# Another order of the same work in the attention and MLP pipeline of a transformer layer on one core

## The chip, the cores and the metric

The kernel runs on 1 core of one Trainium2 chip. The metric is device time of the whole execution in microseconds (us). The core has five engines that run side by side, each through its own list of instructions in order: TensorE (PE, matrix products; its weight loads are listed as PEld), VectorE (DVE), ScalarE (ACT), GpSimd (POOL) and SyncE (SP, which here issues all DMAs). They wait for one another by semaphores only.

## The reference

The input is x of 16 sequences, 1024 positions, 256 channels. Everything is float32.

```python
xn = layernorm(x)                                   # eps 1e-5
Q, K, V = (xn @ W.T + b for W, b in (q, k, v))      # 16 heads of 16 channels
Q, K = rope(Q), rope(K)
scores = where(causal, Q @ K.T / 4, -1e9)           # 1024 x 1024 per head
attn = softmax(scores) @ V @ Wo.T + bo
h = square(relu(xn @ W_fc.T))                       # 1024 hidden channels
y = h @ W_proj.T
spikes = 5 steps of a leaky threshold unit on y     # mem = 0.9 mem + y - reset
out = x + attn + mean(spikes)
```

## The kernel before

The 16 sequences are worked one after another, as 16 *intervals* and a prologue. In interval b the attention of sequence b runs, and beside it the preparation of sequence b+1: layer norm, transposes, queries and keys with rotation, and the MLP. Interval 0 is written out, 1 to 13 are a hardware loop, 14 and 15 are written out again. The prologue has no attention, and interval 15 no next sequence; both use tables of their own for the MLP (MLP_FIRST, MLP_FINAL).

An interval has 18 *steps* n = 0..17, and a step has 5 *places* (n, 0) to (n, 4). Every engine's program walks over the same 90 places, and tables say which piece of work stands at which place. So the order on each engine is fixed by hand. An engine stops at a wait, and all that stands behind it on that engine stops as well.

* Attention goes by 36 *units* of 512 score columns per interval, two per step. PE makes the scores of one half of a unit (2 heads) at the places 0, 1, 3 and 4 (function scores, L1352); I write S16.0 for the first half of unit 16. ACT takes their exponential (L758). There are 2 score buffers, so a half waits until the exponential of the half before the last one is done. POOL masks the diagonal blocks (L664). At place 2 PE multiplies the finished units of earlier steps with the values (a *run*, L1369). The run of step 15 takes (27,0), (28,0), (28,1) and (29,0), where unit 29 is masked at (14, 4).
* T: four transposes of xn into xT (L1132), split by ACT (xT_hi, L715) and DVE (xT_lo, L864) into two parts for products of float32 accuracy.
* QK u.t: the two half-array turns t of query or key block u = 0..3 (query_key, L1152), table QK_AT. DVE rotates it: two operations into rot (L883, L884), two into rot_b (L889, L890); these last two are called rot-odd here. POOL adds (sum_qk, L646), ACT copies the high part to planes (plane_qk), DVE computes the low part into rot_b (low_qk, L894), and SP stores both to memory (store_planes, L423). rot and rot_b have two buffers, u % 2: rot-odd of block 2 waits until the *store* of block 0 has landed (semaphore planes_out, L889's wait), and QK 3.0 on PE waits for rot-odd of block 2.
* SP reads the stored queries and keys back in four quads of heads, 12 + 1 DMAs each (load_ring). The third load of an interval goes to the slot that the first quad used and waits for S8.1.
* M0 to M29: turns of the MLP on PE (L1174 expands, L1183 contracts, 24 matmuls each), table MLP_AT. After an odd turn the next item h is ready: ACT relu (L750), DVE square and high part (L960, L962), POOL low part (h_lo, L656), at the place of RELU_AT, which follows from MLP_AT. M(2k) waits for the h_lo of item k-1. The sums of four items (y) are copied by DVE (take_y, L989) before the next contraction.
* POOL adds the output bias to the residual rows rs (add_bias, L641), once for each of four buffers' turns in an interval. DVE counts the spikes (L971, L974, L982).
* fin/out: PE's output projection of the sequence before (L1114), four times, each followed by DVE's finish (L909) and a DMA (store_out, L480). M2 waits for the last finish.

Of the kernel before, what the change touches and what calls it, by code (L numbers as in the profile page):

```python
# [109 lines left out]
VALUES_AT = {(0, 0): ((0, 0),), (0, 3): ((0, 1), (1, 0)), (1, 0): ((1, 1),), (1, 3): ((2, 0),), (1, 4): ((2, 1),)}  # L110
VALUES_BARE = {(0, 0): ((0, 0),), (0, 3): ((0, 1),), (1, 3): ((2, 0),), (1, 4): ((2, 1),)}
# [17 lines left out]
MLP_AT = {(6, 3): (0,), (7, 0): (1,), (7, 4): (2,), (8, 2): (3, 4), (8, 4): (5, 6), (9, 3): (7, 8), (10, 0): (9,),  # L129
# [9 lines left out]
Y_AT, Y_FIRST = {(10, 0): 0, (13, 0): 1, (16, 0): 2}, {(10, 1): 0, (13, 0): 1}  # L139
# [44 lines left out]
BIAS_HERE_AT, BIAS_NEXT_AT = {(8, 2): (0,), (10, 2): (1,)}, {(14, 2): (0,), (15, 4): (1,)}  # L184
# [28 lines left out]
def layer_kernel(nc, x, wqk, bqk, wv, bv, wfc, wproj, wo, bo, tables, consts, selectors, out):  # L213
    edges = spike_thresholds()
    with ExitStack() as ctx:
# [386 lines left out]
        def _(pool):  # L602
# [64 lines left out]
            def interval(b, att, last, more, norm, first=False, final=False, again=False):  # L667
# [3 lines left out]
                for at in ((n, place) for n in range(NSTEP) for place in range(PLACES)):  # L671
# [13 lines left out]
                    for a in BIAS_HERE_AT.get(at, ()) if att else ():  # L685
                        add_bias(b, 1, a, again)
                    for a in BIAS_NEXT_AT.get(at, ()) if more else ():
                        if first and a == 0:
                            pool.wait_ge(bias_done, 1)
                        add_bias(nb, 0, a, again)  # L690
# [20 lines left out]
        def _(act):  # L711
# [54 lines left out]
            def interval(b, att, last, more, norm, first=False, final=False, again=False):  # L766
# [5 lines left out]
                for at in ((n, place) for n in range(NSTEP) for place in range(PLACES)):  # L772
# [39 lines left out]
        def _(dve):  # L812
# [186 lines left out]
            def interval(b, att, last, more, norm, first=False, final=False, again=False, bare=False):  # L999
# [4 lines left out]
                for at in ((n, place) for n in range(NSTEP) for place in range(PLACES)):  # L1004
# [105 lines left out]
        def _(pe):  # L1110
# [267 lines left out]
            def interval(b, att, last, more, norm, first=False, final=False, again=False):  # L1378
# [6 lines left out]
                for at in ((n, place) for n in range(NSTEP) for place in range(PLACES)):  # L1385
# [115 lines left out]
```

## Time and profile before

| | |
|---|---|
| median of 3 runs | 2238.26 us (2237.26 to 2238.89) |
| the profiled execution's own time | 2238.26 us |
| its span | 2236.5 us |
| PE busy | 2107.6 us, 94% |
| ACT, DVE, POOL busy | 65%, 63%, 50% |
| chain that ended last | PE 64%, issue 10%, POOL 8%, DMA 6%, DVE 5%, ACT 3% |

The span is from the first to the last instruction; 1.8 us of the time lie around it. An interval in the middle takes 132 us, and they follow one another almost identically. Busy shares are of the span. A timeline row has start, duration, engine, line, operation, written tile<-read tiles, shapes and count; what stands in brackets is idle time of the engine before it and what ended that.

### The profile page before, as it was taken

To read this page: it belongs to the slowest core of one execution; us is meant where nothing else is said; L and a number is where in the kernel's file an instruction comes from. 1 tells how busy PE (TensorE), PEld (TensorE's weight loads), DVE (VectorE), ACT (ScalarE), POOL (GpSimd) and SP (SyncE) were. 2 spreads that over 40 slices of the span, in tenths; PEclk is the share of its full clock that TensorE was granted. 3 is DMA by queue.
4 is the path that set the end of the run, shared out by engine and by line. 5 is a ranking of instruction groups with operands and counts; after the bars stand their busy time and mean duration, and the time that the engine had idled before them with its cause. 6 is when DMAs were issued, how large, how long until landed. Compare 5 with 4: busy or idle time off the path is not lost.

```text
span 2236.5 us, 67671 instructions
## 1 busy us (share of the span) xinstructions
PE 2107.6 (94%) x25492; PEld 1511.9 (68%) x25492; DVE 1399.5 (63%) x2134; ACT 1448.7 (65%) x1673; POOL 1122.2 (50%) x1074
## 2 busy tenths in 40 slices
PE   2789999999999999999999999999999999999995
PEld 2657677676767767676776767667676776767653
DVE  5555576684757658576665856667585766857543
ACT  2276766667676666767667676676767666676662
POOL 3445454463645546354564635546464544646341
PEclk9899999999999999999999999999999999999998
DMA  3354453635445363544536455453645536354442
GB/s 127 106 157 112 134 161 92 184 109 162 119 133 169 89 195 102 153 136 116 182 88 188 120 139 150 103 184 95 185 112 137 161 92 185 109 163 119 115 111 69
DMA packets 169850, 299.97 MB, mean 134 GB/s; under 512 B 25088, under 2 KB 114944, under 8 KB 157184
## 3 DMA queue, kind: packets, MB, share of 16 engines
q1 hardware_dynamic: 169600, 296.10, 46.7%
q8 instruction: 222, 3.64, 0.7%
q14 instruction: 28, 0.23, 0.0%
HBM read 174.89 MB, written 103.28 MB: 124 GB/s over the span
## 4 chain that ended last, share of the span: by engine, by line
PE 64%; issue 10%; POOL 8%; DMA 6%; DVE 5%; ACT 3%; SPq 1%; POOLq 0%; DVEq 0%; ACTq 0%
PE pair L1369 17%; PE pair L1174 13%; PE pair L1183 10%; PE pair L1352 10%; PE pair L1152 6%; PE pair L1114 5%; DMA recip_rows<-recip_dram 5%; POOL probs L664 4%; ACT probs L758 3%; PE pair L1166 3%; POOL h_lo L656 2%; POOL rs L641 1%; DMA recip_dram<-denom 1%; DVE rs L982 1%; ACT h_sq L750 1%
## 5 line engine op out<-in xcount | busy, mean ns | idle before, releaser
L758 ACT ACTIVATE probs<-pair 128x1024 f32<-128x1024 f32 x1152 | 1146.3, 1029 | 566.5 <-PE pair L1352 565.6
L656 POOL TENSOR_TENSOR h_lo<-h_sq,h_hi 128x512 fp32r<-128x512 f32 x256 | 396.7, 1549 | 456.8 <-DVE h_hi L962 456.5
L1183 PE MATMUL pair<-wproj_hi,h_hi 64*128 64x256 f32 x2048 | 586.2, 286 | 0.1
L664 POOL TENSOR_SCALAR_AFFINE_SELECT probs<-probs 128x512 f32<-128x512 f32 x512 | 394.0, 787 | 376.6 <-ACT probs L758 374.5
L1174 PE MATMUL pair<-xT_hi,wfc_hi 64*128 64x256 f32 x2048 | 548.3, 287 | 27.6 <-DVE y_sb L989 8.2
L1183 PE MATMUL pair<-wproj_hi,h_lo 64*128 64x256 f32 x2048 | 573.1, 280 | 0.0
L1183 PE MATMUL pair<-wproj_lo,h_hi 64*128 64x256 f32 x2048 | 572.6, 280 | 0.0
L1369 PE MATMUL pair<-probs,v_sb 128*17 128x512 f32 (+3 forms) x6144 | 549.9, 489 | 13.0 <-POOL probs L664 12.1
L1174 PE MATMUL pair<-xT_lo,wfc_hi 64*128 64x256 f32 x2048 | 536.8, 280 | 0.0
L1174 PE MATMUL pair<-xT_hi,wfc_lo 64*128 64x256 f32 x2048 | 536.2, 280 | 0.0
L1352 PE MATMUL pair<-q_ring,k_ring 64*128 64x512 f32 (+3 forms) x3072 | 449.6, 359 | 18.3 <-ACT probs L758 15.4
L1174 PEld LDWEIGHTS pair<-xT_hi,wfc_hi 64*128 64x128 f32 x2048 | 358.9, 187 | 59.2 <-issue 24.4
L960 DVE TENSOR_TENSOR h_sq<-h_sq 128x512 f32<-128x512 f32 x256 | 217.1, 848 | 274.4 <-ACT h_sq L750 271.5
L1183 PEld LDWEIGHTS pair<-wproj_lo,h_hi 64*128 64x128 f32 x2048 | 383.6, 187 | 1.5
L1183 PEld LDWEIGHTS pair<-wproj_hi,h_lo 64*128 64x128 f32 x2048 | 384.0, 188 | 0.0
L1183 PEld LDWEIGHTS pair<-wproj_hi,h_hi 64*128 64x128 f32 x2048 | 382.5, 187 | 0.9 <-issue 0.3
L1352 PEld LDWEIGHTS pair<-q_ring,k_ring 64*128 64x128 f32 x3072 | 258.0, 187 | 181.8 <-ACT probs L758 114.8
L1174 PEld LDWEIGHTS pair<-xT_hi,wfc_lo 64*128 64x128 f32 x2048 | 360.0, 188 | 2.8
L1174 PEld LDWEIGHTS pair<-xT_lo,wfc_hi 64*128 64x128 f32 x2048 | 360.1, 188 | 0.0
L1369 PEld LDWEIGHTS pair<-probs,v_sb 128*17 128x17 f32 x6144 | 150.9, 97 | 289.2 <-issue 233.2
L974 DVE SCALAR_TENSOR_TENSOR count<-y_sb,count 128x512 bf16<-128x512 f32 x256 | 263.8, 1030 | 3.7
L646 POOL TENSOR_TENSOR rot<-rot,rot_b 128x1024 f32<-128x1024 f32 x64 | 153.4, 2397 | 209.0 <-DVE rot_b L890 209.0
(89 smaller groups left out, 2886.9 us busy)
## 6 DMA issues: line engine op xcount, KB each, us to landing
q_ring<-qk_dram SPq DMA_DIRECT2D x384, 128.0 KB
k_ring<-qk_dram SPq DMA_DIRECT2D x384, 128.0 KB
qk_dram<-planes SPq DMA_DIRECT2D x64, 512.0 KB, 2.8
qk_dram<-rot_b SPq DMA_DIRECT2D x64, 512.0 KB, 3.7
xn<-in_x SPq DMA_DIRECT2D x17, 1024.0 KB, 5.7
rs<-in_x SPq DMA_DIRECT2D x64, 256.0 KB, 3.0
acc_dram<-rs SPq DMA_DIRECT2D x64, 256.0 KB, 4.6
attn<-numer SPq DMA_DIRECT2D x256, 64.0 KB, 2.4
```

What stands on the lines that cost most here:

```text
L646: pool.tensor_tensor(rot[u % 2][:, :, :], rot[u % 2][:, :, :], rot_b[u % 2][:, :, :], ALU.add).then_inc(rot_sum, 1)
L656: pool.tensor_tensor(h_lo[i % HB][:, :], h_sq[i % HB][:, :], h_hi[i % HB][:, :].bitcast(F32), ALU.subtract).then_inc(h_lo_done, 1)
L664: ins = pool.affine_select(view, view, [[0, 4], [1, P]], ALU.is_ge, 0.0, base=0, channel_multiplier=-1)
L758: act.activation(probs[BUFFER[n]][:, 2 * pr:2 * pr + 2, :], pair[m % NSLOT][:, :, :], ACT.Exp, scale=SCALE).then_inc(exp_done, 1)
L960: dve.tensor_tensor(sq, sq, sq, ALU.mult).then_inc(sq_h, 1)
L974: dve.scalar_tensor_tensor(count[:, :], y, edges[s], count[:, :], ALU.is_gt, ALU.add).then_inc(spike_step, 1)
L1114: ins = pe.matmul(bank, lhsT, rhs, start=n == 0, stop=n == len(parts) - 1)
L1152: ins = pe.matmul(qk_bank[eo], w[rows, k, m], x[rows, k, cols], start=turn == 0 and n == 0, stop=turn == 1 and n == len(terms) - 1, skip_g ...
L1174: return pe.matmul(fc_bank[i % 2][:, a * T2:(a + 1) * T2], w[rows, k, m], x[rows, k, g * T2:(g + 1) * T2], start=turn == 0 and n == 0, sto ...
L1183: return pe.matmul(proj_bank[:, t * D:(t + 1) * D], h[rows, a * T2 + t * P:a * T2 + (t + 1) * P], w[rows, f, :], start=i % ITEMS_OF_GROUP ...
L1352: ins = pe.matmul(pair[m % NSLOT][:, half, to:to + width(kt, g)], k_ring[rows, slot, pr, kt * P:(kt + 1) * P], q_ring[rows, slot, pr, q0:( ...
L1369: ins = pe.matmul(pv_bank[32 * i:32 * i + VW, q0 - g * G:G], v_sb[:, kt, 4 * quad + i, :], probs[BUFFER[n]][:, i, at:at + width(kt, g)], s ...
```

## The change

Tables and the order of some calls change; no operation is added or removed, and each engine does the same work on the same data.

1. MLP_AT: turns that stood in pairs at one place (7 pairs beside M3 M4, which stay) are put at places of their own, with a score half between them, as in MLP_FIRST. RELU_AT follows. (Y_AT's first entry goes with M9 to (10, 1).)
2. QK_AT: QK 0.1 from (3, 1) to (3, 0); QK 1.0, 2.0 and 3.0 from place 3 to place 4. One value turn goes from (0, 3) to (0, 4).
3. T: the transposes stand behind the run of their step, ACT's copies at place 2 instead of 0, DVE's low part behind take_numer.
4. planes are copied at place 0 of the next step; low_qk of blocks 0 to 2 moves out of the middle of the next rotation to (4, 3), (5, 3), (6, 3).
5. SP: the third ring load goes from step 6 to step 5 and stands ahead of the output store and the store of the planes; the output store stands ahead of the planes in every step.
6. add_bias: both buffers together at (2, 4) and at (13, 4), instead of one each at (8, 2), (10, 2), (14, 2) and (15, 4).

```diff
-VALUES_AT = {(0, 0): ((0, 0),), (0, 3): ((0, 1), (1, 0)), (1, 0): ((1, 1),), (1, 3): ((2, 0),), (1, 4): ((2, 1),)}
+VALUES_AT = {(0, 0): (0, 0), (0, 3): (0, 1), (0, 4): (1, 0), (1, 0): (1, 1), (1, 3): (2, 0), (1, 4): (2, 1)}
...
-QK_AT = {(2, 4): (0, 0), (3, 1): (0, 1), (3, 3): (1, 0), (4, 0): (1, 1), (4, 3): (2, 0), (5, 0): (2, 1),
-         (5, 3): (3, 0), (6, 0): (3, 1)}
+QK_AT = {(2, 4): (0, 0), (3, 0): (0, 1), (3, 4): (1, 0), (4, 0): (1, 1), (4, 4): (2, 0), (5, 0): (2, 1),
+         (5, 4): (3, 0), (6, 0): (3, 1)}
...
-PLANE_AT = {(3, 4): 0, (4, 4): 1, (5, 4): 2, (6, 4): 3}
+PLANE_AT = {(4, 0): 0, (5, 0): 1, (6, 0): 2, (7, 0): 3}
-LOW_QK_AT = {(7, 2): 3}
+LOW_QK_AT = {(4, 3): 0, (5, 3): 1, (6, 3): 2, (7, 2): 3}
...
-MLP_AT = {(6, 3): (0,), (7, 0): (1,), (7, 4): (2,), (8, 2): (3, 4), (8, 4): (5, 6), (9, 3): (7, 8), (10, 0): (9,),
...
+MLP_AT = {(6, 4): (0,), (7, 0): (1,), (8, 0): (2,), (8, 2): (3, 4), (9, 0): (5,), (9, 3): (6,), (9, 4): (7,),
...
-BIAS_HERE_AT, BIAS_NEXT_AT = {(8, 2): (0,), (10, 2): (1,)}, {(14, 2): (0,), (15, 4): (1,)}
+BIAS_HERE_AT, BIAS_NEXT_AT = (2, 4), (13, 4)
...
+                    if att and n == 5:
+                        load_ring(b, d, 2, b * 2 * NUNIT + 2 * NU)
+                    if last and n in (5, 6, 7, 8):
+                        store_out(b - 1, d - 1, n - 5)
                     if more and n in (5, 6, 7, 8):
                         store_planes(nb, nd, n - 5)
-                    if last and n in (5, 6, 7, 8):
-                        store_out(b - 1, d - 1, n - 5)
-                    if att and n == 6:
-                        load_ring(b, d, 2, b * 2 * NUNIT + 2 * NU)
...
-                    for m in T_AT.get(n, ()) if place == 0 and (more or final) else ():
+                    for m in T_AT.get(n, ()) if place == 2 and (more or final) else ():
                         high_xT(tb, m)
...
-                        rotate(nb, u, 0, items_before(b, again) if att else None)
-                        if u:
-                            low_qk(nb, u - 1)
-                        rotate(nb, u, 1, None)
+                        for eo in range(2):
+                            rotate(nb, ROTATE_AT[at], eo, items_before(b, again) if att else None)
...
-                    for m in T_AT.get(n, ()) if place == 2 and (more or final) else ():
-                        transpose(b, tb, m, att, again)
...
                         norms(nb, first_norm_bank if first else norm_bank)
+                    for m in T_AT.get(n, ()) if place == 2 and (more or final) else ():
+                        transpose(b, tb, m, att, again)
```

**SP's DMAs in steps 1 to 8.** These are the rows of interval 0, where no output store stands between. q_ring and k_ring rows with x6 are a ring load, qk_dram rows the store of planes and rot_b. Before:

```order
L432 DMA q_ring<-qk_dram 16x2048 x6
L432 DMA k_ring<-qk_dram 16x2048 x6
L435 DMA q_ring<-shift_dram 2x2048
L423 DMA qk_dram<-planes 128x2x512
L423 DMA qk_dram<-rot_b 128x2x512
L423 DMA qk_dram<-planes 128x2x512
L423 DMA qk_dram<-rot_b 128x2x512
L432 DMA q_ring<-qk_dram 16x2048 x6
L432 DMA k_ring<-qk_dram 16x2048 x6
L435 DMA q_ring<-shift_dram 2x2048
L423 DMA qk_dram<-planes 128x2x512
```

After:

```order
L433 DMA q_ring<-qk_dram 16x2048 x6
L433 DMA k_ring<-qk_dram 16x2048 x6
L436 DMA q_ring<-shift_dram 2x2048
L433 DMA q_ring<-qk_dram 16x2048 x6
L433 DMA k_ring<-qk_dram 16x2048 x6
L436 DMA q_ring<-shift_dram 2x2048
L424 DMA qk_dram<-planes 128x2x512
L424 DMA qk_dram<-rot_b 128x2x512
L424 DMA qk_dram<-planes 128x2x512
L424 DMA qk_dram<-rot_b 128x2x512
```

The 13 DMAs of the third load now stand ahead of the stores of blocks 0 and 1 instead of behind them.

**POOL in steps 12 to 14**, interval 0. AFFINE_SELECT is a mask, h_lo the low part of an MLP item, rs the bias. Before:

```order
L656 TENSOR_TENSOR h_lo_58<-h_sq_50,h_hi_54 128x512
L664 AFFINE_SELECT probs<-probs 128x4x128
L656 TENSOR_TENSOR h_lo_59<-h_sq_51,h_hi_55 128x512
L664 AFFINE_SELECT probs<-probs 128x4x128 x2
L641 TENSOR_TENSOR rs<-rs,bo_sb 128x256 x2
L656 TENSOR_TENSOR h_lo_60<-h_sq_52,h_hi_56 128x512
L664 AFFINE_SELECT probs<-probs 128x4x128 x2
```

After:

```order
L657 TENSOR_TENSOR h_lo_58<-h_sq_50,h_hi_54 128x512
L665 AFFINE_SELECT probs<-probs 128x4x128
L657 TENSOR_TENSOR h_lo_59<-h_sq_51,h_hi_55 128x512
L642 TENSOR_TENSOR rs<-rs,bo_sb 128x256 x4
L665 AFFINE_SELECT probs<-probs 128x4x128 x2
L657 TENSOR_TENSOR h_lo_60<-h_sq_52,h_hi_56 128x512
L665 AFFINE_SELECT probs<-probs 128x4x128 x2
```

The four rs operations stand together and ahead of the masks of unit 28; the last row in both is the mask of unit 29.

**PE in steps 4 to 6**, interval 0: from the run of step 5 to QK 3.0 and the next scores. Before:

```order
L1369 MATMUL pair<-probs,v_sb 17x512 x8
L1369 MATMUL pair<-probs,v_sb 17x256 x4
L1352 MATMUL pair<-q_ring,k_ring 128x256 x4
L1152 MATMUL pair<-xT_hi,wqk_hi 128x512 x2
L1152 MATMUL pair<-xT_hi,wqk_lo 128x512 x2
L1152 MATMUL pair<-xT_lo,wqk_hi 128x512 x2
L1152 MATMUL pair<-xT_hi,wqk_hi 128x512 x2
L1152 MATMUL pair<-xT_hi,wqk_lo 128x512 x2
L1152 MATMUL pair<-xT_lo,wqk_hi 128x512 x2
L1352 MATMUL pair<-q_ring,k_ring 128x256 x4
L1352 MATMUL pair<-q_ring,k_ring 128x512 x2
```

After:

```order
L1369 MATMUL pair<-probs,v_sb 17x512 x8
L1369 MATMUL pair<-probs,v_sb 17x256 x4
L1352 MATMUL pair<-q_ring,k_ring 128x256 x8
L1152 MATMUL pair<-xT_hi,wqk_hi 128x512 x2
L1152 MATMUL pair<-xT_hi,wqk_lo 128x512 x2
L1152 MATMUL pair<-xT_lo,wqk_hi 128x512 x2
L1152 MATMUL pair<-xT_hi,wqk_hi 128x512 x2
L1152 MATMUL pair<-xT_hi,wqk_lo 128x512 x2
L1152 MATMUL pair<-xT_lo,wqk_hi 128x512 x2
L1352 MATMUL pair<-q_ring,k_ring 128x512 x2
```

Both score halves of unit 11 now stand ahead of QK 3.0, and one half behind it.

## Rows read from the trace of the kernel before

**Rows 1.** Busy time by engine of one whole interval, the seventh (busy us, instructions)

```profile
898.53:1030.75 132.22, 129.64 (x1596) 93.19 (x1595) 86.64 (x132) 89.98 (x106) 69.16 (x66) 1.00 0.50 139
```

**Rows 2.** Timeline of SP, steps 4 to 7

```profile
929.32 0.41 SPq L423 DMA_DIRECT2D qk_dram<-planes  x1
929.90 0.39 SPq L423 DMA_DIRECT2D qk_dram<-rot_b  x1
...
940.21 4.29 SPq L432 DMA_DIRECT2D q_ring<-qk_dram  x6
...
949.57 0.39 SPq L423 DMA_DIRECT2D qk_dram<-planes  x1
```

**Rows 3.** DMA issues 905 to 1037 us: KB each, median us to landing

```profile
qk_dram<-planes SPq DMA_DIRECT2D x4, 512.0 KB, 2.8
qk_dram<-rot_b SPq DMA_DIRECT2D x4, 512.0 KB, 3.6
```

**Rows 4.** Timeline of DVE, steps 4 and 5

```profile
930.54 0.69 DVE L909 TENSOR_TENSOR fin<-pair,fin 128x512 f32<-128x512 f32 x1
...
936.70 0.74 DVE L889 SCALAR_TENSOR_TENSOR rot_b<-pair,neg_bqk,table 128x512 f32<-128x512 f32 x1
```

**Rows 5.** Timeline of PE: QK 1.0, S8.1 and QK 3.0

```profile
923.04 0.50 PE L1152 MATMUL pair<-xT_hi,wqk_hi 64*128 64x512 f32 x2 [0.42 <-DVE rot_b L890]
...
926.34 0.39 PE L1352 MATMUL pair<-q_ring,k_ring 64*128 64x512 f32 x2
...
938.91 0.40 PE L1152 MATMUL pair<-xT_hi,wqk_hi 64*128 64x512 f32 x2
```

**Rows 6.** Timeline of PE: one score half between turns; M0, then two halves

```profile
909.19 0.42 PE L1352 MATMUL pair<-q_ring,k_ring 64*128 64x512 f32 x2
909.48 0.39 PE L1166 MATMUL pair<-wv_hi,xT_hi 64*128 64x256 f32 x2
...
946.99 0.28 PE L1174 MATMUL pair<-xT_hi,wfc_hi 64*128 64x256 f32 x2
...
948.42 0.64 PE L1352 MATMUL pair<-q_ring,k_ring 64*128 64x512 f32 x6
948.89 0.34 PE L1174 MATMUL pair<-xT_hi,wfc_hi 64*128 64x256 f32 x2
```

**Rows 7.** Timeline of ACT: the relu behind M21

```profile
1007.46 0.60 ACT L750 ACTIVATE h_sq<-pair 128x512 f32<-128x512 f32 x1 [0.39 <-PE pair L1183]
```

**Rows 8.** Timeline of POOL, step 14

```profile
1007.17 2.31 POOL L641 TENSOR_TENSOR rs<-rs,bo_sb 128x256 f32<-128x256 f32 x2
1009.84 1.67 POOL L656 TENSOR_TENSOR h_lo<-h_sq,h_hi 128x512 fp32r<-128x512 f32 x1 [0.36 <-DVE h_hi L962]
1011.47 2.12 POOL L664 TENSOR_SCALAR_AFFINE_SELECT probs<-probs 128x512 f32<-128x512 f32 x2
```

**Rows 9.** Timeline of PE: the run of step 15

```profile
1010.93 1.92 PE L1369 MATMUL pair<-probs,v_sb 128*17 128x512 f32 x24
1013.65 0.63 PE L1369 MATMUL pair<-probs,v_sb 128*17 128x256 f32 x8 [0.80 <-POOL probs L664]
```

**Rows 10.** Timeline of PE, steps 7 and 8: M2, and S16.0 and S16.1

```profile
955.38 0.38 PE L1174 MATMUL pair<-xT_hi,wfc_hi 64*128 64x256 f32 x1 [0.19 <-DVE fin L909]
...
957.49 0.50 PE L1352 MATMUL pair<-q_ring,k_ring 64*128 64x512 f32 x2 [0.18 <-ACT probs L758]
```

**Rows 11.** Timeline of DVE, the copy of y ahead of M10

```profile
974.59 1.67 DVE L982 SCALAR_TENSOR_TENSOR rs<-count,rs 128x512 f32<-128x512 bf16 x1
976.18 0.68 DVE L989 COPY y_sb<-pair 128x512 f32<-128x512 f32 x1
```

**Rows 12.** Busy time and granted clock (PEclk, behind POOL) around an idle PE and after

```profile
51.00:55.00 4.00, 0.05 (x4) 0.04 (x2) 3.86 (x5) 0.37 (x1) 0.01 (x1) 0.90 0.11 41
55.00:60.00 5.00, 4.94 (x22) 3.46 (x24) 0.00 (x0) 2.00 (x2) 5.00 (x2) 0.50 0.48 177
...
2122.70:2126.10 3.40, 3.40 (x25) 0.62 (x16) 0.78 (x1) 0.81 (x1) 3.03 (x5) 0.50 0.00 0
```

More of the change, by code:

```diff
@@ L109 @@
 PLACES = 5
-VALUES_AT = {(0, 0): ((0, 0),), (0, 3): ((0, 1), (1, 0)), (1, 0): ((1, 1),), (1, 3): ((2, 0),), (1, 4): ((2, 1),)}
-VALUES_BARE = {(0, 0): ((0, 0),), (0, 3): ((0, 1),), (1, 3): ((2, 0),), (1, 4): ((2, 1),)}
+VALUES_AT = {(0, 0): (0, 0), (0, 3): (0, 1), (0, 4): (1, 0), (1, 0): (1, 1), (1, 3): (2, 0), (1, 4): (2, 1)}
+VALUES_BARE = {(0, 0): (0, 0), (0, 3): (0, 1), (1, 3): (2, 0), (1, 4): (2, 1)}
 TAKE_V_AT = {(0, 3): (0,), (1, 0): (1,), (1, 4): (2, 3)}
@@ L138 @@
              (13, 3): (13,), (14, 0): (14,), (14, 3): (15,), (15, 0): (16,), (15, 3): (17,)}
-Y_AT, Y_FIRST = {(10, 0): 0, (13, 0): 1, (16, 0): 2}, {(10, 1): 0, (13, 0): 1}
+Y_AT, Y_FIRST = {(10, 1): 0, (13, 0): 1, (16, 0): 2}, {(10, 1): 0, (13, 0): 1}
 Y_FINAL = {(11, 3): 2, (15, 3): 3}
@@ L684, in interval @@
                         h_low(item, i)
[L685 to L688, printed above, removed]
+                    if att and at == BIAS_HERE_AT:
+                        for a in range(2):
+                            add_bias(b, 1, a, again)
+                    if more and at == BIAS_NEXT_AT:
+                        if first:
                             pool.wait_ge(bias_done, 1)
-                        add_bias(nb, 0, a, again)
+                        for a in range(2):
+                            add_bias(nb, 0, a, again)
             root(0)
@@ L1011, in interval @@
                         take_numer(b - 1, *NUMER_AT[n], last)
-                    for m in T_AT.get(n, ()) if place == 2 and (more or final) else ():
-                        low_xT(tb, m)
                     if att and n and place == 2 and n in NUMER_AT:
@@ L1019, in interval @@
                         divide(b - 1, 1)
+                    for m in T_AT.get(n, ()) if place == 2 and (more or final) else ():
+                        low_xT(tb, m)
                     if more and at in ROTATE_AT:
-                        u = ROTATE_AT[at]
-                        if first and u == 0:
+                        if first and ROTATE_AT[at] == 0:
                             dve.wait_ge(table_in, 16)
                             dve.wait_ge(consts_done, 2)
-                        rotate(nb, u, 0, items_before(b, again) if att else None)
-                        if u:
-                            low_qk(nb, u - 1)
-                        rotate(nb, u, 1, None)
+                        for eo in range(2):
+                            rotate(nb, ROTATE_AT[at], eo, items_before(b, again) if att else None)
                     if last and place == 2 and n in O_AT:
@@ L1388, in interval @@
                         scores(b, 2 * n + place // 3, place % 3, last, more)
-                    for m in T_AT.get(n, ()) if place == 2 and (more or final) else ():
-                        transpose(b, tb, m, att, again)
                     if last and at == (0, 2):
@@ L1398, in interval @@
                         norms(nb, first_norm_bank if first else norm_bank)
+                    for m in T_AT.get(n, ()) if place == 2 and (more or final) else ():
+                        transpose(b, tb, m, att, again)
                     if last and place == 2 and n in O_AT:
                         output(b - 1, O_AT[n])
-                    for m, turn in values_at.get(at, ()) if att else ():
+                    if att and at in values_at:
+                        m, turn = values_at[at]
                         if carried and m < CARRIED:
```

7 rows, old and new, of the table MLP_AT are left out of this document.

## The prediction, made before the changed kernel ran

> **What bounds the kernel now.** I read the page first: PE busy 94%, no other engine above 65%. Then one interval of the middle by busy time: PE works 129.6 of 132.2 us at a granted clock of 1.00 [rows 1], so its idle time is only 2.6 us. PE's own order of work is the bound, and no engine beside it is near it. What the change does to PE is then two things: whether its pieces fit together more or less tightly, and whether a wait that is now covered comes uncovered. Third, I went through PE's timeline of that interval and took the distance from each piece's start to the next. A piece that is not kept waiting has always the same length: M0 goes from 946.99 to 948.42, which is 1.43 us [rows 6], and so does every MLP turn; runs, outputs and QK turns have theirs. All that stands above these lengths is about 5 us an interval. The largest waits are 0.6 us ahead of QK 1.0 (0.42 of it shown as idle, behind rot_b) [rows 5], 0.6 us ahead of M2 for the last finish and 0.4 us ahead of S16.1 [rows 10], 1.1 us ahead of M10 for the copy of y [rows 11], and 1.0 us inside the run of step 15 for a mask [rows 9]. So even an order without any waits could not win more than 5 us x 15 = 75 us. Fourth, since PE waits for DVE, DVE for stores, and SP issues them in order, I read SP's timeline.
>
> Times below are those of the seventh interval, with the changed order laid over them. The tables changed act in intervals 0 to 14, so each term counts 15 times.
>
> **The third ring load ahead of the stores.** It can't start before S8.1, which is at 926.34 and takes 0.4 us [rows 5]; in the new order about 0.3 us later by the pieces ahead of it, so the issue starts at about 927.1. How long does SP take for it? In the trace the load starts at 940.21 and the next DMA behind it at 949.57: 9.36 us for 13 DMAs [rows 2]. The output store (its finish is done by 931.2 [rows 4]) comes next, and each issue takes 0.58 us (929.32 to 929.90 [rows 2]). So planes go out at 937.1 and rot_b at 937.7, and rot_b lands after 3.6 us [rows 3]: 941.3. Before, the same store was issued at 929.32 and had landed by 933.5. Rot-odd of block 2 waits for this landing; it started at 936.70 and takes two operations of 0.7 us, 1.4 us [rows 4]. It will now start at 941.4 and end at 942.8. QK 3.0 started at 938.91 [rows 5] and with the score half put ahead of it would be due at 939.3. It waits 3.5 us. Queued behind rot-odd on DVE are a copy of the numerator, the finish of output 1, low_qk 1 and the rotation of block 3; on POOL the sum of block 2; all of them are needed only behind QK 3.0, so they move along and add 0.2 us at most (M0 waits for block 3). Term: +3.5 us, from 0 (if the store came through in time) to 5 (if the ring's data delays its landing).
>
> Moving low_qk 0 behind the finish at 930.54 [rows 4] would alone be hidden: done at 932.5, issued at once, landed at 936.9, two tenths behind 936.70 and ahead of 939.3.
>
> Here the Trainium skill speaks for the change. "DMA: Bandwidth & Descriptors", in its rules for kernel authors, says to issue a DMA early and wait for it late. By that rule the earlier ring load costs nothing, and the sum would be 3.5 us an interval lower. The same page, on the anatomy of one DMA, gives some 50 ns for the dispatch by the issuing sequencer (for GpSimd's path); 13 of them would be 0.7 us, with the same result. This case's rows show 0.7 us for each DMA of a ring load on SP, 9.36 us in all [rows 2].
>
> **Pairs of turns taken apart.** On PE the 72 score halves stand in 50 groups now and in 59 then. A group of one half between turns takes 0.29 us (909.19 to 909.48), a group of two 0.47 us (948.42 to 948.89) [rows 6]; ahead of a run one half takes 0.32. So each group more costs 0.11 to 0.19 us. 9 x 0.15 = +1.35 us (1.0 to 1.7).
>
> **The run of step 15.** Its last part needs the mask of unit 29, which on POOL stands behind the low part of item 11, which begins with M21. M21 ends at 1007.3, its relu starts at 1007.46 [rows 7], h_lo ends at 1011.5, the mask at 1013.6 [rows 8], and the last part of the run starts at 1013.65 [rows 9]. That chain of 6.3 us stays. But between M21 and the run one MLP turn fewer stands then (M22 alone, where M22 and M23 stood): 1.43 us less cover. Term at least +1.4. And POOL now does both bias pairs behind h_lo 10. A pair took 2.31 us [rows 8]. Counting from the end of M19: h_lo 10 done at 3.5, bias at 8.1, the two masks of unit 28 at 9.8, h_lo 11 at 11.5, mask 29 at 13.6, run done at 14.2; without a wait it would be done at 10.2. That is 4.0 us of waiting, against 1.0 before: +3.0. If the pairs take less, as they should with DVE less busy, nearer to 1.4. I take the middle, +2.2 us.
>
> **Three score halves in a row.** M2 goes behind S16.0 and M5 behind S18.0. The third half in a row must wait for an exponential (0.93 to 1.03 us) of the first. For M2: S16.0 comes about 1.0 us late, while the 0.6 us for the finish and the 0.4 us for S16.1 [rows 10] are gone: 0. For M5: S18.0 about 1.1 us late; the 0.4 us ahead of M6 (h_lo 2) goes. Together +0.8 us (0 to 1.5).
>
> **Transposes behind the run.** The chain transpose, xT_hi, xT_lo, QK 0.0 has lost the run's 2.28 us as cover and keeps QK 0.0 waiting 0.9 us. Then QK 1.0, whose rotation hangs on the reciprocal's DMA and comes at 923.0 whatever PE does, no longer waits 0.6 us [rows 5], and a 0.3 us wait ahead of QK 0.1 goes. Term 0 (-0.3 to +0.5).
>
> **The copy of y.** It waited behind a 1.67 us operation on rs that ended late (974.59, copy at 976.18 [rows 11]); in the new order one score half more lies between, and DVE is through. -0.5 us (-0.6 to 0). The bias at (2, 4) is hidden: POOL would wait there for the rotation of block 0, and the four operations (4.6 us at most [rows 8]) end about when that does; half a microsecond more would only delay a sum that is due a step later.
>
> Sum per interval: 3.5 + 1.35 + 2.2 + 0.8 + 0 - 0.5 = 7.35 us; x 15 = 110 us.
>
> **The clock.** In the middle of the kernel the clock was granted in full [rows 1]. PE now gets a hole of 3.5 us. Where PE stood still for 4 us in the prologue (51 to 55), the clock fell to 0.50, that is 1.2 GHz, and the turns after it ran at that [rows 12]; and in interval 15, where PE's waits are longer than in the middle ones, there is a stretch of 3.4 us at 0.50 [rows 12]. 3.4 us at half speed do the work of 1.7, so a fall costs up to 1.7 us. The seventh interval, with waits of 1 us at most, has none [rows 1]. I take one fall per interval, mostly behind QK 3.0: +1.5 us (0 to 3.4, if the run of step 15 brings another), x 15 = 22 us.
>
> Own time of the profiled execution 2238.3 (span 2236.5 and 1.8 around it), which is the median of the runs: 2238.3 + 110 + 22 = **2370 us**.
>
> **Rivals.**
> - *No fall of the clock.* For it: no stall of the middle intervals had one. Against: none was this long. 2238.3 + 110 = 2348 us.
> - *The ring load doesn't hold up the stores*, the case of the rule above: if SP gets through it sooner, or the landing is in time. For: rot-odd is only due at 937.9, and the DMA engines are only half busy [rows 1]. Against: 9.36 us of issue. Sum 7.35 - 3.5 = 3.85 us, no hole, no fall of the clock: 2296 us.
> - *Both waits at their upper end*: ring data delays the landing (+1.5), the bias holds the mask (+0.8), and the clock falls twice (+1.7): 13 us an interval, 2430 us.
> - *Faster.* Turns spread evenly give the chain behind each turn more time, and the waits of today go: 0.6 + 0.6 + 0.4 + 0.4 + 0.5 + 1.0 = 3.5 us, less 1.0 for the groups: -2.5 us x 15, 2201 us. It needs the store in time, and it is decided at step 15: the mask would have to be done before the run gets to it, 3 us earlier than I count. Against: the chain of M21 is 6.3 us by rows, and the cover I count is less than it.
>
> **How the numbers follow.** Forecast 0.40, no fall 0.27, ring load harmless 0.16, upper end 0.08, faster 0.04, nearly nothing 0.02, and 0.03 for something slower that I don't see. The likeliest is 2370 us. The range goes from 2293 (ring load harmless) to 2402 and leaves out the upper end and the faster side. A change of 0.2% (4.5 us) is about what can be told here. Slower by more: 0.94; within: 0.02; faster: 0.04.
>
> **What would show it.** In the changed profile rot-odd of block 2 should be released by a DMA (qk_dram<-planes or rot_b) and QK 3.0 by it, with 3 to 4 us of idle PE in every interval and a step 5 near 12 us; SP should show planes of block 0 issued some 10 us behind S8.1. The run of step 15 should take over 4.5 us, released by POOL. PEclk should fall below 1.00 in the middle slices. I am wrong if the planes are stored in time, or if DVE shows no wait there; and if intervals stay near 132 us, the view that PE's waits are the price of the order is wrong.

## The result and the profile after

| | before | changed |
|---|---|---|
| median | 2238.57 us | 2439.39 us (2433.15 to 2440.19, 4 runs) |
| span of the profiled execution | 2236.5 us | 2434.8 us |
| mean granted clock | 0.988 | 0.962 |
| PE busy | 94% | 90% |

The ratio is 1.089, with a 95% interval of 1.087 to 1.091. The change costs 201 us, 13.4 us for each of 15 intervals (12.4 us in the seventh, 975.10 to 1119.71). The forecast was 2370 us with a range to 2402: the sign was right, the size half as large again as forecast.

The span in 40 slices, busy tenths of PE: first the row of the page before, then two rows of the changed kernel's page, PE and tenths of the granted clock:

```profile
PE   2789999999999999999999999999999999999995
```

```profile
PE   3889999898989989999898989989999898999985
PEclk9899999999999999999999999999999999999998
```

PE's row, which was all nines in the middle, has eights now. The clock's row has nines as before: tenths of a slice are too coarse for what the mean clock shows. From 0.988 to 0.962 is 131 us more at half speed (0.038 x 2434.8 x 2 = 185 us, less 0.012 x 2236.5 x 2 = 54 us). At half speed that is work worth up to 66 us. PE's busy time grew by 77 us (2107.6 to 2184.2) and its idle time by 122 us (128.9 to 250.6).

The waits that grew, over the whole trace of the changed kernel (total us, times, longest us):

```profile
DVE rot_b L892 <- DMA qk_dram<-rot_b: 121.5, 31, 7.8
...
PE pair L1152 <- DVE rot_b L893: 79.6, 18, 6.4
```

Before, the first did not occur, and the second was this:

```profile
PE pair L1152 <- DVE rot_b L890: 18.4, 16, 4.0
```

The groups of the page, with idle time behind the second bar, show the other two places: the run (L1369) and the score halves (L1352). Before:

```profile
L1369 PE MATMUL pair<-probs,v_sb 128*17 128x512 f32 (+3 forms) x6144 | 549.9, 489 | 13.0 <-POOL probs L664 12.1
...
L1352 PE MATMUL pair<-q_ring,k_ring 64*128 64x512 f32 (+3 forms) x3072 | 449.6, 359 | 18.3 <-ACT probs L758 15.4
```

Changed:

```profile
L1369 PE MATMUL pair<-probs,v_sb 128*17 128x512 f32 (+3 forms) x6144 | 556.9, 492 | 43.5 <-POOL probs L665 41.1
...
L1352 PE MATMUL pair<-q_ring,k_ring 64*128 64x512 f32 (+3 forms) x3072 | 473.0, 360 | 41.9 <-ACT probs L761 41.8
```

**The ring load and the store, steps 4 and 5 of the seventh interval.** SP's timeline of the changed kernel, which answers to [rows 2]:

```profile
1004.03 3.85 SPq L433 DMA_DIRECT2D q_ring<-qk_dram  x6
1008.06 3.80 SPq L433 DMA_DIRECT2D k_ring<-qk_dram  x6
1012.04 0.52 SPq L436 DMA_DIRECT2D q_ring<-shift_dram  x1
1012.79 0.41 SPq L481 DMA_DIRECT2D out<-fin  x1
1013.64 0.40 SPq L424 DMA_DIRECT2D qk_dram<-planes  x1
1014.22 0.37 SPq L424 DMA_DIRECT2D qk_dram<-rot_b  x1
```

DVE's timeline in that stretch (low_qk of block 0, then rot-odd of block 2), to [rows 4]:

```profile
1008.20 1.64 DVE L897 TENSOR_TENSOR rot_b<-rot,planes 128x1024 fp32r<-128x1024 f32 x1
...
1019.55 0.75 DVE L892 SCALAR_TENSOR_TENSOR rot_b<-pair,neg_bqk,table 128x512 f32<-128x512 f32 x1 [6.77 <-DMA qk_dram<-rot_b]
```

PE's, from the score halves of unit 11 to QK 3.0, to [rows 5]:

```profile
1015.70 0.74 PE L1352 MATMUL pair<-q_ring,k_ring 64*128 64x256 f32 x8
1021.01 0.79 PE L1152 MATMUL pair<-xT_hi,wqk_hi 64*128 64x512 f32 x2 [4.58 <-DVE rot_b L893]
```

Read them from the bottom. PE stands still for 4.58 us. DVE has stood still for 6.77 us before that, for a store. SP had the data at 1009.84, when low_qk ended, but it was in the middle of 13 DMAs and issued the store at 1013.64. From the last issue to the release are 5.3 us (1014.22 to 1019.55), where I had counted 3.6. From the load's first row to the release are 15.5 us, where I had counted 14.2 (927.1 to 941.3).

**The run of step 15.** POOL's timeline, to [rows 8], and PE's, to [rows 9]:

```profile
1088.16 2.19 POOL L657 TENSOR_TENSOR h_lo<-h_sq,h_hi 128x512 fp32r<-128x512 f32 x1 [1.65 <-DVE h_hi L965]
1090.31 3.46 POOL L642 TENSOR_TENSOR rs<-rs,bo_sb 128x256 f32<-128x256 f32 x4
1093.72 1.86 POOL L665 TENSOR_SCALAR_AFFINE_SELECT probs<-probs 128x512 f32<-128x512 f32 x2
1095.55 1.70 POOL L657 TENSOR_TENSOR h_lo<-h_sq,h_hi 128x512 fp32r<-128x512 f32 x1
1097.21 2.13 POOL L665 TENSOR_SCALAR_AFFINE_SELECT probs<-probs 128x512 f32<-128x512 f32 x2
```

```profile
1094.47 2.22 PE L1369 MATMUL pair<-probs,v_sb 128*17 128x512 f32 x24
1099.39 1.06 PE L1369 MATMUL pair<-probs,v_sb 128*17 128x256 f32 x8 [2.69 <-POOL probs L665]
```

POOL has no idle time from h_lo 10 to the mask of unit 29: h_lo 10, the four bias operations, masks, h_lo 11, masks. That chain ends at 1099.3. From the run's start to the next score half (1094.47 to 1100.37) are 5.9 us, where it was 3.3 us (1010.93 to 1014.20).

**The clock.** Stretches of the changed kernel behind the two holes (columns as in [rows 12]; the clock is the third number from the end):

```profile
1020.70:1024.10 3.40, 3.09 (x14) 2.24 (x16) 3.40 (x4) 0.00 (x0) 3.06 (x2) 0.51 0.23 77
...
1099.20:1102.60 3.40, 3.21 (x26) 2.29 (x28) 1.29 (x2) 1.02 (x1) 0.13 (x1) 0.51 0.65 188
```

There are two falls in this interval, and read in stretches of 3 us the trace shows these two in each of the 15 intervals. I had forecast one. The chip granted 1.2 GHz behind the 4.58 us without matmuls and behind the 2.69 us in the run.

### The profile page after: what moved, and what is told of

Same layout as the page of the kernel before. It is cut to its first block and busy times, and to the rows that moved or that the text cites. A ratio compares the mean times of both kernels' runs of the same rounds, so it can differ in the third digit from the quotient of the medians.

```text
span 2434.8 us, 67671 instructions
## 1 busy us (share of the span) xinstructions
PE 2184.2 (90%) x25492; PEld 1553.9 (64%) x25492; DVE 1431.1 (59%) x2134; ACT 1462.3 (60%) x1673; POOL 1122.6 (46%) x1074
## 5 line engine op out<-in xcount | busy, mean ns | idle before, releaser
L657 POOL TENSOR_TENSOR h_lo<-h_sq,h_hi 128x512 fp32r<-128x512 f32 x256 | 382.7, 1495 | 614.1 <-DVE h_hi L965 613.7
L1183 PE MATMUL pair<-wproj_hi,h_hi 64*128 64x256 f32 x2048 | 604.3, 295 | 0.1
L1369 PE MATMUL pair<-probs,v_sb 128*17 128x512 f32 (+3 forms) x6144 | 556.9, 492 | 43.5 <-POOL probs L665 41.1
L665 POOL TENSOR_SCALAR_AFFINE_SELECT probs<-probs 128x512 f32<-128x512 f32 x512 | 417.6, 833 | 358.8 <-ACT probs L761 358.7
L1174 PE MATMUL pair<-xT_hi,wfc_hi 64*128 64x256 f32 x2048 | 563.1, 294 | 16.0 <-DVE y_sb L992 5.3
L1174 PE MATMUL pair<-xT_lo,wfc_hi 64*128 64x256 f32 x2048 | 545.3, 285 | 0.0
L1352 PE MATMUL pair<-q_ring,k_ring 64*128 64x512 f32 (+3 forms) x3072 | 473.0, 360 | 41.9 <-ACT probs L761 41.8
L1174 PEld LDWEIGHTS pair<-xT_hi,wfc_hi 64*128 64x128 f32 x2048 | 368.5, 192 | 56.5 <-issue 17.7
L1352 PEld LDWEIGHTS pair<-q_ring,k_ring 64*128 64x128 f32 x3072 | 265.4, 190 | 186.7 <-ACT probs L761 111.3
L963 DVE TENSOR_TENSOR h_sq<-h_sq 128x512 f32<-128x512 f32 x256 | 196.5, 767 | 302.1 <-ACT h_sq L753 301.0
L1174 PEld LDWEIGHTS pair<-xT_hi,wfc_lo 64*128 64x128 f32 x2048 | 369.3, 193 | 5.1
L1369 PEld LDWEIGHTS pair<-probs,v_sb 128*17 128x17 f32 x6144 | 149.7, 97 | 329.1 <-issue 229.4
L977 DVE SCALAR_TENSOR_TENSOR count<-y_sb,count 128x512 bf16<-128x512 f32 x256 | 293.7, 1147 | 4.7
```

What stands on the lines that cost most here:

```text
L657: pool.tensor_tensor(h_lo[i % HB][:, :], h_sq[i % HB][:, :], h_hi[i % HB][:, :].bitcast(F32), ALU.subtract).then_inc(h_lo_done, 1)
L665: ins = pool.affine_select(view, view, [[0, 4], [1, P]], ALU.is_ge, 0.0, base=0, channel_multiplier=-1)
L963: dve.tensor_tensor(sq, sq, sq, ALU.mult).then_inc(sq_h, 1)
L977: dve.scalar_tensor_tensor(count[:, :], y, edges[s], count[:, :], ALU.is_gt, ALU.add).then_inc(spike_step, 1)
L1174: return pe.matmul(fc_bank[i % 2][:, a * T2:(a + 1) * T2], w[rows, k, m], x[rows, k, g * T2:(g + 1) * T2], start=turn == 0 and n == 0, sto ...
L1183: return pe.matmul(proj_bank[:, t * D:(t + 1) * D], h[rows, a * T2 + t * P:a * T2 + (t + 1) * P], w[rows, f, :], start=i % ITEMS_OF_GROUP ...
```

## The experiments

All were timed against the kernel before; two of them are variants of the changed kernel. In the expectations "Theory A" is the account of the prediction, sized with the changed kernel's trace: a store queued on SP behind a ring load, a mask that PE reaches too soon, and a clock that falls behind the holes.

### Change 5 alone

```diff
+                    if att and n == 5:
+                        load_ring(b, d, 2, b * 2 * NUNIT + 2 * NU)
+                    if last and n in (5, 6, 7, 8):
+                        store_out(b - 1, d - 1, n - 5)
                     if more and n in (5, 6, 7, 8):
                         store_planes(nb, nd, n - 5)
-                    if last and n in (5, 6, 7, 8):
-                        store_out(b - 1, d - 1, n - 5)
-                    if att and n == 6:
-                        load_ring(b, d, 2, b * 2 * NUNIT + 2 * NU)
```

> The kernel before with change 5 alone: SP issues the third ring load at step 5, ahead of the output store and the store of the planes. Theory A (the queue): rotation of block 2 waits for a store that is issued 9 us late. By the changed kernel's trace (planes issued 9.6 us behind the load's start, 5.2 us from the last issue to the release) rot-odd of block 2 ends about 4.7 us after QK 3.0 is due, and the clock falls behind the hole: +6 to +7 us an interval, 2330 to 2345 us. Rival B (the wait comes from low_qk being moved behind the finish, and the ring load is hidden): below +1 us an interval, under 2255 us.

Measured: 2334.0 us, ratio 1.043 (1.041 to 1.044), +95 us. Its SP, DVE, PE and clock:

```profile
961.07 4.95 SPq L432 DMA_DIRECT2D q_ring<-qk_dram  x6
966.20 3.80 SPq L432 DMA_DIRECT2D k_ring<-qk_dram  x6
...
972.37 0.37 SPq L423 DMA_DIRECT2D qk_dram<-rot_b  x1
```

```profile
976.12 0.75 DVE L889 SCALAR_TENSOR_TENSOR rot_b<-pair,neg_bqk,table 128x512 f32<-128x512 f32 x1 [5.23 <-DMA qk_dram<-rot_b]
```

```profile
977.58 0.80 PE L1152 MATMUL pair<-xT_hi,wqk_hi 64*128 64x512 f32 x2 [4.41 <-DVE rot_b L890]
```

```profile
977.58:982.00 4.42, 4.42 (x22) 3.59 (x24) 1.14 (x2) 1.03 (x2) 2.37 (x1) 0.50 0.51 177
```

Here low_qk stands where it did before, and the hole is as large. So SP's new order alone is sufficient; rival B falls. Of the 95 us, 57 are more idle time of PE (128.9 to 185.7 us) and 38 more busy time (2107.6 to 2146.0). The mean clock of 0.971 is 82 us more at half speed, worth up to 41, so the fall behind the hole is enough to account for the busy part.

The store lands sooner here than in the changed kernel: 3.75 us from the last issue (972.37) to the release (976.12), and 3.6 to 3.9 us in 13 of the 15 intervals, against 4.5 to 5.8 there in all but the first. It stands behind the same 13 DMAs. So the long landing in the changed kernel does not come of the ring load ahead of it alone; what else makes it was not found. In return SP took longer to issue here (5.13 us for the first six, 4.03 there), and from the load's first row to the release are 15.1 us.

### The changed kernel without change 5

> The changed kernel with SP's order of before (changes 1 to 4 and 6 stay). Theory A: the 4.7 us hole ahead of QK 3.0 and the fall of the clock behind it go, 6 to 7 us an interval: 2335 to 2350 us. Rival B: nearly all of the hole stays, over 2420 us.

Measured: 2367.0 us, ratio 1.058 (1.056 to 1.059). Taking change 5 out gives back 72 us, less than the 89 to 104 of theory A, and far more than rival B allows. The hole ahead of QK 3.0 is gone, but DMAs still release waits (whole trace):

```profile
DVE rot_b L890 <- DMA qk_dram<-rot_b: 65.5, 30, 3.1
...
ACT h_sq L751 <- DMA qk_dram<-rot_b: 21.4, 15, 2.7
```

Behind the first of these waits PE stands ahead of M0 (0.73 us in the seventh interval):

```profile
PE pair L1173 <- DVE rot_b L891: 16.4, 16, 3.1
```

There was a second instance of the same mechanism, which changes 2 and 4 alone show below. In the changed kernel PE's wait ahead of M0 for rot_b occurs twice in the whole trace, and the relu's wait for a DMA three times (3.5 us in all): with change 5 the hole ahead of QK 3.0 takes their place.

### Change 1 alone, the turns apart

> The kernel before with change 1 alone (the MLP turns of the changed kernel, relu and h_lo follow). Theory A: more groups of score halves (+1.0 to 1.4 us), M2 and M5 behind a third half (+0.8), M10's wait shorter (-0.5), and in the run of step 15 one turn less of cover (+1.4), with no more than 1.7 for a fall of the clock: +2.5 to +5 us an interval, 2275 to 2315 us. Rival (even spacing helps and the bias makes the wait of step 15): +0 to +1 us an interval, under 2255 us.

Measured: 2303.6 us, ratio 1.029 (1.028 to 1.031), +65 us, 4.3 us an interval. The last part of its run of step 15 waits longer than before:

```profile
1038.25 0.98 PE L1370 MATMUL pair<-probs,v_sb 128*17 128x256 f32 x8 [2.05 <-POOL probs L665]
```

This wait stands in every interval. Behind it the clock fell in 11 of 15 (read in stretches of 3 us, granted clock below 0.9).

### Change 6 alone, the bias pairs

```diff
-BIAS_HERE_AT, BIAS_NEXT_AT = {(8, 2): (0,), (10, 2): (1,)}, {(14, 2): (0,), (15, 4): (1,)}
+BIAS_HERE_AT, BIAS_NEXT_AT = {(2, 4): (0, 1)}, {(13, 4): (0, 1)}
```

> The kernel before with change 6 alone: both bias pairs at (2, 4) and at (13, 4). Theory A: in the old order of turns POOL has room at (13, 4) (it waits 1.9 us there for h_hi), so mask 29 is not later: -0.5 to +0.5 us an interval, 2231 to 2246 us. Rival (the bias holds up the masks whatever the turns do): +1 to +2 us an interval, 2253 to 2268 us.

Measured: 2242.7 us, ratio 1.0019 (1.0009 to 1.0029): +4 us, inside theory A's range. In the old order of turns the bias is nearly free.

### Changes 1 and 6 together

> The kernel before with changes 1 and 6 together. Alone they cost 65 us and 4 us. Theory A (step 15: with the turns apart, PE gets to the run before the mask, and then the bias pair ahead of the masks on POOL is late too): the wait in the run grows by 0.7 to 1.2 us against the turns alone, and the clock falls behind it in more intervals: 2318 to 2340 us. Rival (the two add up, the bias has no part in the wait): 2303 to 2310 us.

Measured: 2323.9 us, ratio 1.038 (1.036 to 1.040), +86 us, where the two alone make 69. The wait in the run is 2.69 us as in the changed kernel:

```profile
1051.18 0.86 PE L1370 MATMUL pair<-probs,v_sb 128*17 128x256 f32 x8 [2.69 <-POOL probs L665]
```

So, in this pair of kernels, the bias costs 20 us where POOL's chain is the one that PE waits for, and 4 us where it isn't.

### Change 1, but with the old places of M19 to M24

```diff
-          (12, 0): (14,), (12, 3): (15,), (12, 4): (16,), (13, 0): (17,), (13, 3): (18,), (13, 4): (19,),
-          (14, 0): (20,), (14, 3): (21,), (15, 0): (22,), (15, 3): (23,), (15, 4): (24,),
+          (12, 0): (14,), (12, 3): (15,), (12, 4): (16,), (13, 0): (17,), (13, 3): (18,), (14, 0): (19, 20),
+          (14, 3): (21, 22), (15, 0): (23,), (15, 3): (24,),
```

> Change 1 alone as in the run with the turns apart, but M19 to M24 at their places of before: pairs at (14, 0) and (14, 3), M23 at (15, 0). Theory A (of its 65 us more than half is the run of step 15, 1 us more of waiting and the clock that falls behind the 2.05 us hole): 2.2 to 3.0 us an interval less, 2258 to 2272 us, and no stretch at 0.50 in the middle intervals. Rival (the cost is that of the single groups everywhere): one group fewer, 0.2 us an interval less, 2298 to 2304 us.

Measured: 2261.5 us, ratio 1.010 (1.008 to 1.013). Six turns at their old places give back 42 of the 65 us. The interval's clock is full again:

```profile
909.82:1043.55 133.73, 130.30 (x1596) 93.33 (x1595) 85.40 (x132) 90.57 (x105) 67.95 (x66) 1.00 0.48 137
```

What is left, 23 us or 1.6 us an interval, is the price of more groups, of the third halves and of M10's shorter wait. PE's order in the trace has 49 groups of score halves in an interval before, 54 here, 56 with change 1 whole and 58 in the changed kernel. So there are five groups more here, at 0.15 us 0.75 us, and the prediction's terms come to 0.75 + 0.8 - 0.5 = 1.05 us. The third halves cost more than counted. PE waits 0.89 us for the exponential at each of two; here and before:

```profile
PE pair L1353 <- ACT probs L759: 40.3, 45, 1.7
```

```profile
PE pair L1352 <- ACT probs L758: 15.4, 30, 1.7
```

### Changes 2 and 4 alone

> The kernel before with changes 2 and 4 alone: QK turns at other places, planes a place later, low_qk behind the finish; SP's order stays. Theory A: the rotation of block 2 comes in time, but low_qk of block 2 is later by 3 us and its store waits behind the ring load of step 6, so the relu of item 1 is held by a DMA: +0.5 to +2.5 us an interval, 2246 to 2276 us. Rival (all of it is hidden): 2233 to 2244 us.

Measured: 2271.3 us, ratio 1.015 (1.014 to 1.017), +33 us, the upper third of theory A. SP's order is that of before, and yet (whole trace):

```profile
DVE rot_b L889 <- DMA qk_dram<-rot_b: 66.0, 30, 3.2
...
ACT h_sq L750 <- DMA qk_dram<-rot_b: 14.1, 14, 1.4
```

Rot-odd now waits twice an interval for a landing, for blocks 0 and 1, and the relu for the store of block 2, which stands behind the ring load of step 6. PE feels both: it waits 0.99 us ahead of M0 for the rotation of block 3, and 1.30 us at a score half, whose exponential stands behind the relu on ACT. These 2.3 us agree with the 2.2 us an interval of the result. In the seventh interval:

```profile
966.15 0.60 ACT L750 ACTIVATE h_sq<-pair 128x512 f32<-128x512 f32 x1 [1.02 <-DMA qk_dram<-rot_b]
966.64 2.85 ACT L758 ACTIVATE probs<-pair 128x1024 f32<-128x1024 f32 x3
```

### Change 2 alone

```diff
-QK_AT = {(2, 4): (0, 0), (3, 1): (0, 1), (3, 3): (1, 0), (4, 0): (1, 1), (4, 3): (2, 0), (5, 0): (2, 1),
-         (5, 3): (3, 0), (6, 0): (3, 1)}
+QK_AT = {(2, 4): (0, 0), (3, 0): (0, 1), (3, 4): (1, 0), (4, 0): (1, 1), (4, 4): (2, 0), (5, 0): (2, 1),
+         (5, 4): (3, 0), (6, 0): (3, 1)}
```

> The kernel before with the places of the QK turns of the changed kernel alone (change 2); planes and low_qk stay. Theory A (of the 33 us of changes 2 and 4 together it is the late low_qk, which makes the stores of blocks 1 and 2 late, that costs): -0.3 to +0.6 us an interval, 2233 to 2247 us. Rival (the later QK turns cost by themselves): 2258 to 2271 us.

Measured: 2239.8 us, ratio 0.9998 (0.9988 to 1.0008). The QK turns are free where they stand; the 33 us belong to change 4, the later planes and low_qk, at least beside change 2. Change 4 was not run alone, nor planes and low_qk apart.

### Change 3 alone

> The kernel before with change 3 alone: transposes behind the run, xT_hi at place 2, xT_lo behind take_numer. Theory A: QK 0.0 waits about 1 us, and of that 0.3 to 0.6 come back ahead of QK 1.0: +0 to +0.7 us an interval, 2238 to 2250 us. Rival (the transposes are free wherever they stand): 2234 to 2242 us.

Measured: 2243.3 us, ratio 1.003 (1.002 to 1.004), +5 us or 0.35 us an interval: PE waits 1.02 us for xT_lo ahead of QK 0.0, as counted, and gets back the most of it.

### The changed kernel, ring load behind the planes

```diff
-                    if att and n == 5:
-                        load_ring(b, d, 2, b * 2 * NUNIT + 2 * NU)
-                    if last and n in (5, 6, 7, 8):
-                        store_out(b - 1, d - 1, n - 5)
                     if more and n in (5, 6, 7, 8):
                         store_planes(nb, nd, n - 5)
+                    if att and n == 5:
+                        load_ring(b, d, 2, b * 2 * NUNIT + 2 * NU)
+                    if last and n in (5, 6, 7, 8):
+                        store_out(b - 1, d - 1, n - 5)
```

> The changed kernel with one edit: at step 5 the order is store of the planes, ring load, output store (the load stays at step 5). Theory A (the queue, whichever store is behind the load): block 0 is stored in time and the 4.7 us hole ahead of QK 3.0 goes, but now the store of block 1 is behind the load, rotation of block 3 waits for its landing and PE stands 2 to 3 us ahead of M0: 2385 to 2415 us. Rival (only the store of block 0 matters): as without change 5, 2360 to 2370 us.

Measured: 2415.8 us, ratio 1.080 (1.078 to 1.082), 0.8 us above the range of theory A. SP's timeline and the waits of the whole trace:

```profile
999.29 0.39 SPq L424 DMA_DIRECT2D qk_dram<-rot_b  x1
1000.02 4.44 SPq L433 DMA_DIRECT2D q_ring<-qk_dram  x6
...
1010.43 0.37 SPq L424 DMA_DIRECT2D qk_dram<-planes  x1
```

```profile
PE pair L1173 <- DVE rot_b L891: 57.3, 16, 4.6
```

24 us of the 72 come back. The hole has moved: PE waits ahead of M0 (L1173 is the expansion) instead of QK 3.0, because now it is the store of block 1 that is issued behind the load.

### Half of the ring load first

```diff
+                    if att and n == 5:
+                        load_ring(b, d, 2, b * 2 * NUNIT + 2 * NU, (0,))
                     if more and n in (5, 6, 7, 8):
                         store_planes(nb, nd, n - 5)
...
                     if att and n == 6:
-                        load_ring(b, d, 2, b * 2 * NUNIT + 2 * NU)
+                        load_ring(b, d, 2, None, (1, 2))
```

> The kernel before, with the 6 q_ring DMAs of the third ring load at step 5 ahead of the store of the planes, and the 6 k_ring and 1 shift DMAs where the load was. Theory A (what counts is SP's issue time ahead of the store, 0.7 us a DMA): 4.2 us of issue instead of 9.2, the planes are issued at 931.1 instead of 929.3 on the scale of the seventh interval and land by 936.8, when rot-odd is due: -0.3 to +0.6 us an interval, 2233 to 2248 us, and no hole. Rival (the ring's data on the DMA engines, or the early load in itself, delays the stores in proportion): half of the cost of the whole load, 2275 to 2290 us.

Measured: 2239.0 us, ratio 0.9998 (0.9988 to 1.0008). Six DMAs ahead of the store cost nothing. All thirteen, with the output store ahead as well, cost 95 us. The price starts somewhere between, where the slack of the rotation ends.

### Two waits taken out

```diff
-INVERT_LAST, DIVIDE_LAST, INVERT_AT, DIVIDE_AT = (1, 3), (3, 0), (11, 0), (14, 0)
+INVERT_LAST, DIVIDE_LAST, INVERT_AT, DIVIDE_AT = (1, 3), (3, 2), (11, 0), (14, 0)
...
-SPIKES_HERE = {(8, 3): (0, 0), (8, 4): (0, 1), (9, 1): (0, 2), (9, 2): (0, 3), (9, 3): (0, 4), (9, 4): (0, 5),
+SPIKES_HERE = {(8, 3): (0, 0), (8, 4): (0, 1), (9, 0): (0, 2), (9, 1): (0, 3), (9, 2): (0, 4), (9, 3): (0, 5),
```

> The kernel before with DVE's order changed at two places: the division by the softmax sum behind the rotation of block 0 ((3, 0) to (3, 2)), and the third to sixth spike operation one place earlier, so that the rs operation is at (9, 3) and not ahead of the copy of y. Theory A (PE's waits are the price of the order, and each may be taken out by itself): QK 1.0 and M10 come up to 0.5 us sooner each, -0.5 to -1.1 us an interval, 2222 to 2231 us. Rival (the half microseconds come back in the next wait): 2235 to 2241 us.

Measured: 2226.3 us, ratio 0.9945 (0.9932 to 0.9957), 0.8 us an interval. This is faster than both kernels. Its DVE and PE around QK 1.0:

```profile
915.45 0.74 DVE L890 SCALAR_TENSOR_TENSOR rot_b<-pair,bqk_sb,table 128x512 f32<-128x512 f32 x1
916.11 0.68 DVE L864 TENSOR_TENSOR xT_lo<-pair,xT_hi 128x512 fp32r<-128x512 f32 x1
916.71 3.05 DVE L904 TENSOR_TENSOR attn<-attn,recip_rows 128x1024 f32<-128x1024 f32 x1
```

```profile
915.78 0.50 PE L1352 MATMUL pair<-q_ring,k_ring 64*128 64x512 f32 x2
916.24 0.50 PE L1152 MATMUL pair<-xT_hi,wqk_hi 64*128 64x512 f32 x2
```

QK 1.0 follows the score half after 0.46 us, where it was 0.92 (922.12 to 923.04). The division, which waits for a DMA, no longer stands ahead of the rotation. Over the whole trace PE's waits for rot_b at L1152 fall from 18.4 to 12.7 us, and those for the copy of y from 8.2 to 0.8 us.

## Why the prediction was right and where it was wrong

**The bound, right.** PE's own order sets the time. Taking waits out of it by DVE's order alone gave 12 us; putting waits in cost up to 95.

**Where the 69 us are.** Three of the kernels are nested, and each step can be held against the prediction's terms for it:

| step | forecast | measured |
|---|---|---|
| changes 1 and 6 | (1.35 + 2.2 + 0.8 - 0.5) x 15 = 58 us | 86 us |
| and 2, 3, 4 and the value turn (the changed kernel without change 5) | 0 | 43 us (2367.0 less 2323.9) |
| and 5 | 3.5 x 15 + 22 = 75 us | 72 us |

(Of the nine groups in the term 1.35, two belong to the second step, 4 to 5 us.) The shortfall is 28 + 43 - 3 = 68 us. It does not lie in the ring load, on which the forecast rested, but in the part that was to give 2296 us without it and gave 2367. Two steps of the prediction failed: low_qk put at nothing (changes 2 and 4 alone cost 33 us), and the clock put at one fall an interval of 1.5 us (there are two; worth up to 66 us against 22).

**The third ring load, mechanism right.** Forecast 3.5 us, measured 4.58 us of idle time in the seventh interval. The issue of 13 DMAs and the place of the store came as counted (9.6 us from the load's first row to planes). The landing was longer, 5.3 us against 3.6, and was not explained: with change 5 alone it was mostly 3.6 to 3.9 us, and PE's hole 4.41 us even so. That the hole comes of the issue order, and not of low_qk, is shown by change 5 alone (+95 us) and by the half load (0). The rival that the load is harmless falls with it. That this step's total came out within 3 us is partly luck: alone, the change costs 95 us, 20 more than forecast, and beside the others 23 less than that, since it takes the place of waits that changes 2 and 4 had made.

**low_qk "would alone be hidden", wrong.** I followed block 0 only, and for that block the store does not hold up PE. Changes 2 and 4 alone cost 33 us, change 2 alone nothing. Blocks 1 and 2 are stored later too, and the store of block 2 comes behind the ring load of step 6. PE then waits ahead of M0 and at a score half, 2.3 us together.

**The run of step 15, waiting right, price wrong.** Forecast +2.2 us, measured 5.9 against 3.3 us, +2.6. Both causes are shown: putting M19 to M24 back makes the wait 0.81 us again, as before (0.80), and the bias makes it longer only with the turns apart. But with its fall of the clock, and two groups more, this place costs 62 us (2323.9 less 2261.5), where 2.2 x 15 = 33 us and 4 to 5 us for the groups were forecast.

**The groups, the third halves and the copy of y, near.** With M19 to M24 at their old places 1.05 us were forecast and 1.6 us measured. The third halves were counted too low (+0.8 us for both; PE waits 0.89 us at each). **The transposes**: 0 forecast, 0.35 us measured, inside -0.3 to +0.5.

**The clock, wrong in number and size.** Forecast one fall an interval, 22 us in all; the measured mean clock means 131 us more at 0.50, worth up to 66 us of PE's work. There are two falls an interval, and I had put the second, behind the run, among the upper ends. The kernel with changes 1 and 6, where only the run has a long wait, has a mean clock of 0.978: 48 us more at half speed than before, worth up to 24. With change 1 but M19 to M24 at their old places there is no fall in the interval shown. With change 1 alone the 2.05 us already cost clock in 11 of 15 intervals.

**The range, wrong by that.** The rival "both waits at their upper end", 2430 us, comes nearest, and it had a chance of 0.08. It is right in the second fall, the longer landing and the late mask; but it too had low_qk at nothing, so that its number fits is partly luck. The mistake was to treat its parts as separate accidents: in the changed kernel both waits and both falls stand in every interval.

The single changes cost 95 (5), 65 (1), 33 (2 and 4), 5 (3) and 4 us (6), 202 in all. That this meets the measured 201 is partly chance, since changes 1 and 6 add 17 us to each other and change 5 costs 23 us less beside the others. The move of one value turn to (0, 4) was not run alone.

**The Trainium skill.** "DMA: Bandwidth & Descriptors" says, in its rules for kernel authors, to issue a DMA early and wait for it late. This case's runs don't bear it out where one queue carries both a bulk load and a store that someone waits for: the load came a step earlier and cost 95 us, 6.3 us an interval, and half of it earlier won nothing.

## What to carry to other kernels

Before a DMA is moved forward, count what it puts itself ahead of on its issuing queue, in issue time, and compare that with the slack of whoever waits for what stands behind. When a kernel is bound by one engine's order, look for the few places where another engine's chain ends just in time; a piece of cover removed there costs its whole length and more (one turn of 1.43 us, or 21 us in 15 intervals, cost 42 us here, some 4 of them for two groups more), while elsewhere the same kind of move is cheap or free. Where a stall of TensorE is forecast, size the fall of its clock with it.

## What the runs showed of the hardware that I had not expected

Waits of PE inside a run can be followed by the lower clock as the long hole is: 2.69 us was followed by 0.51 in the stretch shown, while the 1.02 us ahead of QK 0.0 in every interval of the transposes' run left the clock at its level of before (mean 0.988). It is not certain behind a given wait, and the longer wait did not have more falls: 2.05 us in every interval with change 1 alone, with a fall in 11 of 15; 2.69 us with changes 1 and 6 (in the seventh), with a fall in 10 of 15.

And the division L904 took 3.05 us where it started beside POOL's sum, which was already running (916.27 to 918.67 with two waits taken out), and 1.22 us before, where POOL's h_lo started just behind it; there h_lo took 2.18 us. Since nothing waited for the division, its 3.05 us cost nothing.
